# Two graph attention layers, 16 batches on one core: five places in another order, and the third values from rounded halves

## The chip, the core and the metric

The kernel runs on one core of a Trainium2 chip. Such a core has a matrix engine (TensorE, here PE, with its weight loads as PEld), a vector engine (DVE), a scalar engine (ACT), GpSimd (POOL) and a sequencer that only issues transfers (SyncE, SP). They run side by side and wait for each other through semaphores. The metric is the device time of one launch in microseconds, lower is better.

## The reference, cut to what matters

There are 16 batches of 512 nodes with 256 features. Each batch goes through a graph attention network of two layers (four heads, then one), a residual sum and a norm, and then through a third attention layer, a second residual and norm:

```python
def gat_layer(x, mask, W, a_src, a_dst, bias, concat):
    xl = (x @ W).reshape(B, N, H, F)
    asrc = jnp.einsum('bnhf,hf->bnh', xl, a_src)
    adst = jnp.einsum('bnhf,hf->bnh', xl, a_dst)
    e = leaky_relu(asrc[:, :, None, :] + adst[:, None, :, :], 0.2)
    e = jnp.where(mask[..., None], e, -1e9)
    attn = jax.nn.softmax(e, axis=1)          # over the sources
    out = jnp.einsum('bsdh,bshf->bdhf', attn, xl)
...
x1 = layernorm(x + gat_layer(elu(gat_layer(x, 4 heads)), 1 head))
Wh = x1 @ W                                   # the "third values"
e = leaky(s_i + s_j), masked; attention = softmax(e, axis=1)
out = layernorm(x1 + leaky(attention @ Wh))
```

## The kernel before

**Tiles.** The 512 nodes are four blocks of 128 partitions, and an attention map is a tile `att` of 128 x (4 x 512), three of them in turn. One map is a *unit*: a head ("h", four per batch), the second layer ("L2") or the third ("L3").

**The steady part.** Units are put into slots, six to a batch: in round n position 0 holds L3 of batch n-3, positions 1 to 4 the heads 0 to 3 of batch n, position 5 L2 of batch n-1. Each engine runs one loop over the slots (PE line 662, ACT 838, DVE 1171, POOL 431), and the order of the instructions within a slot is written out by hand, for each engine apart. Nothing reorders them: an engine that waits holds up all that stands behind.

**What a unit passes through.** PE spreads the source scores over PSUM (`sources_row`, L470 into bA). DVE takes the masked maxima over it (`tops`, four passes, L942), and from them the shifted targets (`shifted_targets`: low L955, b_t L960). PE spreads b_t (`targets_row`, L470 into bB). ACT applies the leaky slope (`leaky`, L734, two pairs) and the exponential (`exps`, L749). DVE clears what is no edge (`keep_edges`, L993). In the next slot PE multiplies the map with the values, in two halves (`attend`; heads L510, L2 L521, L3 L531). A head then goes through `invert` (DVE, L973), `normalize` (ACT, L761), `elu_exp` (ACT, L769), `elu` (DVE, L967), `turn_head` (PE, four transposes, L500), `high_part` (ACT, L775) and `low_part` (DVE, L979). The last L2 but one is already taken through exps and keep_edges in two halves (`halved_second`).

**Values.** The first values (`values_1`, L618 and L621) and the second (`values_2`, L603) are made of three matmuls each in a rounded format (fp32r): high x high, high x low, low x high. The third values (`values_3`, L591) are one full-precision product for each of two blocks of the contraction, which the profile shows as two matmul instructions. Before them `turn_x1` transposes x1 on PE (L582), and `x1_out` copies it out on ACT (L785). Products go through two banks bG; ACT copies them out (`values_1_out` L802, `values_2_out` L797, `values_3_out` L792).

**PE's order** in the positions that matter here, in round n:
- position 5: values_1 block 2; attend head 3, first half; turn_head; values_1 block 3; attend, second half; sources_row
- position 0: turn_x; attend L2, first half; turn_head; targets_row; attend L2, second half; sources_row
- position 1: attend L3, first half; turn_head; targets_row of head 1; values_1 block 0; attend L3, second half; sources_row
- position 3: values_2 blocks 2 and 3; attend head 1, first half; targets_row of head 3; turn_x1; attend, second half; sources_row of L2
- position 4: values_3 blocks 0 and 1; attend head 2, first half; turn_head; targets_row of L2; values_3 blocks 2 and 3; attend, second half; sources_row

**The rest.** `second_out` (DVE, L1020 and L1023) takes the second layer out of PSUM in two pairs and adds x; the statistics of both norms are `norm_stats` (DVE, L1032 and L1035), for the third layer at the end of position 4. POOL adds the bias to x (`add_bias_2`, L407), sets the diagonal (L421), adds the second residual (L429), writes the second norm (L390) and scales the third values (`scale_3`, L415). x_low (L1003) and make_mask (L998) run on DVE in position 0. After slot 96 comes a tail in which the last batch's layers follow one another with little beside them.

## Time and profile before

| | |
|---|---|
| median of three runs | 938.67 us (938.52 to 939.26) |
| the profiled execution | 939.34 us, span 937.1 us |
| granted TensorE clock, mean | 0.987 of full |
| PE busy | 874.0 us, 93% |
| PE's weight loads | 815.5 us, 87% |
| DVE busy | 753.4 us, 80% |
| ACT busy | 687.4 us, 73% |
| POOL busy | 258.1 us, 28% |
| moved by DMA | 45.03 MB |

Busy times overlap, so they don't add up. A matmul's end is modelled and reaches into the next one, so the distance between two starts tells what a group of matmuls takes, not the sum of their durations. The timeline merges instructions of one line that follow each other, and the bracket behind a row says how long the engine stood still before it and what it waited for.

### The profile page before, as it was taken

What the parts mean: (1) busy time and instruction counts of PE and PEld (TensorE: products, weight loads), DVE (VectorE), ACT (ScalarE), POOL (GpSimd) and SP (SyncE); (2) the same over time, 40 slices, a digit from 0 to 9 for tenths busy, and PEclk for the clock granted to TensorE, in tenths of its full rate; (3) what the DMA queues carried; (4) which work ended last, traced back from release to release, by engine and by line L of the source; (5) the groups of instructions that cost most, each with busy time, mean ns of one, the idle gap of its engine ahead of it and who ended that gap; (6) DMA issues with size and microseconds to landing.
All of it is one profiled execution on the core that took longest, in us unless ns stands there. A gap on an engine that the chain in (4) does not pass through costs nothing.

```text
span 937.1 us, 17310 instructions
## 1 busy us (share of the span) xinstructions
PE 874.0 (93%) x6220; PEld 815.5 (87%) x6220; DVE 753.4 (80%) x1908; ACT 687.4 (73%) x1274; POOL 258.1 (28%) x244
## 2 busy tenths in 40 slices
PE   6779889999999999999999999999999999999887
PEld 4778889998989989899998989999898998989775
DVE  6876788888788888878888887888888788887666
ACT  2686769687786877778687777868788686887653
POOL 1001020133242312434231243323224332332512
PEclk9898999999999999999999999999999999999999
DMA  7032030303013040300303021030301101000002
GB/s 217 25 106 76 1 90 2 90 2 111 3 33 81 3 111 2 85 30 25 89 1 113 2 48 65 23 92 1 114 1 46 68 23 23 1 24 1 24 1 68
DMA packets 62747, 45.03 MB, mean 48 GB/s; under 512 B 35780, under 2 KB 54340, under 8 KB 62664
## 3 DMA queue, kind: packets, MB, share of 16 engines
q1 hardware_dynamic: 62664, 43.93, 16.5%
q8 instruction: 51, 0.84, 0.4%
q14 instruction: 32, 0.26, 0.1%
HBM read 27.14 MB, written 8.39 MB: 38 GB/s over the span
## 4 chain that ended last, share of the span: by engine, by line
PE 38%; DVE 30%; ACT 23%; issue 9%; POOL 0%; DMA 0%; DVEq 0%; SPq 0%; POOLq 0%; ACTq 0%
DVE junk L942 9%; PE bUU L510 8%; PE bUU L531 7%; PE bG L603 6%; PE bG L621 6%; ACT att L734 5%; ACT att L749 5%; ACT x L761 4%; DVE y_lo L979 3%; PE bB L470 3%; DVE low L955 3%; DVE y L967 3%; DVE att L993 2%; ACT att L753 2%; DVE stats L1032 2%
## 5 line engine op out<-in xcount | busy, mean ns | idle before, releaser
L510 PE MATMUL bUU<-val,att 128*128 128x129 f32 x2048 | 249.2, 275 | 0.3 <-DVE att L993 0.3
L942 DVE CUSTOM_DVE_ANT_0 junk<-mask_t,bA,val 128x512 bf16<-128x512 bf16 x320 | 219.9, 743 | 33.9 <-PE bA L470 30.1
L510 PEld LDWEIGHTS bUU<-val,att 128*128 128x128 f32 x2048 | 241.4, 192 | 2.3 <-issue 0.5
L993 DVE SCALAR_TENSOR_TENSOR att<-mask_n,att 128x2048 f32<-128x2048 bf16 x78 | 178.8, 2292 | 79.3 <-ACT att L749 79.1
L734 ACT ACTIVATE att<-bB,val 128x512 f32<-128x512 f32 x320 | 202.7, 708 | 5.4 <-PE bB L470 5.4
L749 ACT ACTIVATE att<-att 128x2048 f32<-128x2048 f32 x78 | 151.5, 1942 | 0.6
L521 PE MATMUL bUU<-val,att 128*128 128x257 f32 x480 | 109.8, 381 | 1.9 <-DVE att L989 1.2
L531 PE MATMUL bUU<-val3s,att 128*128 128x256 f32 x480 | 109.2, 381 | 1.7 <-DVE res L1023 0.2
L381 POOL TENSOR_SCALAR var_eps<-moments 128x4 f32<-128x4 f32 x29 | 5.7, 195 | 368.1 <-DVE moments L1035 368.1
L802 ACT COPY val<-bG 128x524 f32<-128x524 f32 x62 | 37.6, 606 | 93.3 <-PE bG L621 93.3
L761 ACT ACTIVATE x<-bUU,zinv 128x128 f32<-128x128 f32 x256 | 73.4, 375 | 43.8 <-DVE zinv L973 43.8
L531 PEld LDWEIGHTS bUU<-val3s,att 128*128 128x128 f32 x480 | 89.1, 190 | 15.6 <-issue 4.0
L521 PEld LDWEIGHTS bUU<-val,att 128*128 128x128 f32 x480 | 88.7, 190 | 14.4 <-DVE att L989 1.5
L390 POOL TENSOR_SCALAR act<-res,moments,rstd 128x256 f32<-128x256 f32 x52 | 87.7, 1696 | 1.5
L603 PE MATMUL bG<-w_hi,y_hi 128*128 128x258 f32 x256 | 75.3, 294 | 0.3 <-DVE y_lo L979 0.3
L603 PE MATMUL bG<-w_hi,y_lo 128*128 128x258 f32 x256 | 72.4, 283 | 0.0
L621 PE MATMUL bG<-w_hi,x_hi 128*128 128x262 f32 x248 | 72.4, 292 | 0.0
L621 PE MATMUL bG<-w_lo,x_hi 128*128 128x262 f32 x248 | 72.3, 292 | 0.0
L603 PE MATMUL bG<-w_lo,y_hi 128*128 128x258 f32 x256 | 72.3, 282 | 0.0
L621 PE MATMUL bG<-w_hi,x_lo 128*128 128x262 f32 x248 | 72.1, 291 | 0.0
L470 PE MATMUL bB<-ident,b_t 128*128 128x128 f32 x320 | 50.7, 282 | 21.2 <-DVE b_t L960 21.1
L415 POOL TENSOR_SCALAR val3s<-val,z3inv 128x256 f32<-128x256 f32 x60 | 38.5, 657 | 98.3 <-DVE z3inv L1010 95.3
(126 smaller groups left out, 1635.8 us busy)
## 6 DMA issues: line engine op xcount, KB each, us to landing
adj_in<-in_adj_dram SPq DMA_DIRECT2D x16, 1024.0 KB, 5.8
x_in<-in_x_dram SPq DMA_DIRECT2D x16, 512.0 KB, 6.7
out_dram<-act SPq DMA_DIRECT2D x14, 512.0 KB, 2.9
mask_t<-mask_n SPq DMA_TRANSPOSE x64, 2.5
att<-in_L_gnn_W_dram SPq DMA_DIRECT2D x4, 128.0 KB, 3.1
val<-in_L_gnn_W_dram SPq DMA_DIRECT2D x1, 512.0 KB, 7.2
out_dram<-x_in SPq DMA_DIRECT2D x1, 512.0 KB, 2.9
w<-in_L_gnn_W_dram SPq DMA_DIRECT2D x1, 256.0 KB, 7.4
```

Of the source, the lines that this page charges most:

```text
L390: nc.gpsimd.tensor_scalar(act3[:, b], res2[:, b], moments[:, 1, b, 0:1], rstd[:, 1, b:b + 1], ALU.subtract, ALU.mult).then_inc(y_out_done, 1)
L470: ins = nc.tensor.transpose(bank[:, b * P:(b + 1) * P], column(b).to_broadcast([P, P]), ident[:])
L510: ins = nc.tensor.matmul(to[:, (d % 2) * FX:(d % 2 + 1) * FX], p[:, s, d * P:(d + 1) * P], val1[u.batch % 2][:, s, u.index // 2, values], ...
L521: ins = nc.tensor.matmul(to[:, 0:DO + 1], p[:, s, d * P:(d + 1) * P], val2[:, s, 2:DX + 1], start=(s == 0), stop=(s == NB - 1))
L531: ins = nc.tensor.matmul(to[:, d * DO:(d + 1) * DO], p[:, j, (2 * i + d) * P:(2 * i + d + 1) * P], val3s[:, j], start=(j == 0), stop=(j == ...
L603: ins = nc.tensor.matmul(g_bank(b % 2)[:, 0:DX], left[:, k, nodes], right[:, k], start=(k == 0 and i == 0), stop=(k == KH - 1 and i == 2))
L621: ins = nc.tensor.matmul(to, left[:, k, nodes], right[:, k, g], start=False, stop=(k == KD - 1 and i == 2))
L734: nc.scalar.activation(p[:, b], bB[:], ACT.Prelu, bias=a_col(u, b), alpha=SLOPE)\
L749: nc.scalar.activation(flat(p), flat(p), ACT.Exp).then_inc(exp_done, 1)
L761: nc.scalar.activation(x1[u.h % 2][:, d * P:(d + 1) * P], bU[u.use[d // 2] % 4][:, (d % 2) * FX:(d % 2) * FX + F], ACT.Copy, scale=zinv[u. ...
L942: nc.vector.tensor_tensor_reduce(junk[:, b] if u.row else att[u.slot % 3][:, b], mask_t[u.batch % 4][:, b], bA[:], 1.0, a_col(u, b) if u.r ...
L993: nc.vector.scalar_tensor_tensor(flat(p), mask_n[u.batch % 3][:, 0:NB * N], BIG, flat(p), ALU.add, ALU.min)\
```

## The change

1. ACT, position 5: `values_1_out` of block 2 stands before the second pair of leaky, not behind it.
2. DVE, position 1: the second pair of `second_out` stands behind tops and shifted_targets of the next head.
3. DVE: `norm_stats` of the third layer goes from the end of position 4 to position 5, behind invert.
4. POOL, position 3: `add_bias_2` waits until b_t of head 3 is there. POOL's order stays.
5. Every L2 is taken through exps and keep_edges in two halves, and attend waits for its own half; attend of L3 waits for the third values block by block.
6. Third values as three fp32r products. ACT rounds x1 (x1_hi), DVE subtracts (`x1_low`: x1_lo) in position 3, behind keep_edges, and twice in the tail. w3 is split once, at the start, by two more DVE instructions. PE waits for all of x1_lo before the first block.

The tiles and semaphores that the diff declares are left out here.

```diff
@@ -63,15 +63,19 @@
 
-    halved_second = units[LAST - 1]
     PARTS = (range(0, 2), range(2, 3), range(3, 4))
...
         u.r = i
+
+    pieces = 0
     for u in units.values():
         u.h = H * u.batch + u.index
+        u.p = pieces
+        if u.row:
+            pieces += 1 if u.kind == "h" else NB if u is final_second else 2
 
...
@@ -441,6 +451,8 @@
                 if pos == 3 and 0 <= n - 1 < B:
+
+                    pool.wait_ge(b_t_ready, units[SLOTS * n + H].r + 1)
                     add_bias_2(n - 1)
@@ -504,7 +516,7 @@
                 to = u_bank(u.use[i])
-                pe.wait_ge(prob_done, u.r + 1)
+                pe.wait_ge(prob_done, u.p + 1)
                 for d in range(2 * i, 2 * i + 2):
@@ -514,7 +526,7 @@
                 p = att[u.slot % 3]
-                pe.wait_ge(prob_done, u.r + 1 + (i if u is halved_second else 0))
+                pe.wait_ge(prob_done, u.p + i + 1)
                 for d in range(2 * i, 2 * i + 2):
@@ -525,9 +537,10 @@
                 to = u_bank(u.use[i])
-                pe.wait_ge(val3s_done, (u.batch + 1) * NB)
                 for d in range(2):
                     for j in range(NB):
+                        if i == 0 and d == 0:
+                            pe.wait_ge(val3s_done, u.batch * NB + j + 1)
                         ins = nc.tensor.matmul(to[:, d * DO:(d + 1) * DO], p[:, j, (2 * i + d) * P:(2 * i + d + 1) * P],
@@ -536,7 +549,7 @@
                 for s in sources:
-                    pe.wait_ge(prob_done, u.r + s + 2)
+                    pe.wait_ge(prob_done, u.p + s + 1)
                     for d in range(NB):
@@ -581,15 +594,16 @@
                     ins.then_inc(x1t_turned, 1)
-                    g_free[k] = ((x1t_ready, m * KD + k + 1),)
+                    g_free[k] = ((x1_hi_ready, m * KD + k + 1), (x1_lo_ready, m + 1))
 
...
                     g_wait(b % 2)
+                    pe.wait_ge(x1_lo_ready, m + 1)
                     for k in range(KD):
-                        pe.wait_ge(x1t_ready, m * KD + k + 1)
-                        ins = nc.tensor.matmul(g_bank(b % 2)[:, 0:DX], x1_t[:, k, b * P:(b + 1) * P], w3[:, k],
-                                               start=(k == 0), stop=(k == KD - 1))
+                        for i, (left, right) in enumerate(((x1_hi, w3_hi), (x1_hi, w3_lo), (x1_lo, w3_hi))):
+                            ins = nc.tensor.matmul(g_bank(b % 2)[:, 0:DX], left[:, k, b * P:(b + 1) * P], right[:, k],
+                                                   start=(k == 0 and i == 0), stop=(k == KD - 1 and i == 2))
                     ins.then_inc(val3_done, 1)
@@ -676,6 +690,8 @@
                 if pos == 4 and third:
+                    if n == 2:
+                        pe.wait_ge(w3_lo_ready, 1)
                     values_3(n - 2, (0, 1))
@@ -740,7 +756,7 @@
                 p = att[u.slot % 3]
-                if u is halved_second:
+                if u.kind == "L2":
                     act.wait_ge(leaky_done, (u.u + 1) * NB)
@@ -782,7 +798,7 @@
                     act.wait_ge(x1t_turned, m * KD + k + 1)
-                    nc.scalar.copy(x1_t[:, k], g_bank(k)).then_inc(x1t_ready, 1)
+                    nc.scalar.copy(x1_hi[:, k], g_bank(k)).then_inc(x1_hi_ready, 1)
 
@@ -853,6 +869,8 @@
                     normalize(older)
+                if pos == 5 and batch:
+                    values_1_out(n + 1, 2)
                 if this:
@@ -861,8 +879,6 @@
                     values_3_out(n - 2, (0, 1))
-                if pos == 5 and batch:
-                    values_1_out(n + 1, 2)
                 if this:
@@ -982,14 +998,14 @@
                 dve.wait_ge(diag_done, u.batch + 1)
-                if u is halved_second:
+                if u.kind == "L2":
                     mask = mask_n[u.batch % 3][:, 0:NB * N].rearrange("p (b n) -> p b n", n=N)
                     for i, half in enumerate((slice(0, N // 2), slice(N // 2, N))):
-                        dve.wait_ge(exp_done, u.r + i + 1)
+                        dve.wait_ge(exp_done, u.p + i + 1)
                         nc.vector.scalar_tensor_tensor(p[:, :, half], mask[:, :, half], BIG, p[:, :, half], ALU.add, ALU.min)\
...
                     return
-                dve.wait_ge(exp_done, u.r + 1)
+                dve.wait_ge(exp_done, u.p + 1)
                 nc.vector.scalar_tensor_tensor(flat(p), mask_n[u.batch % 3][:, 0:NB * N], BIG, flat(p), ALU.add, ALU.min)\
@@ -1002,6 +1018,11 @@
                                         x_hi[:].rearrange("p k n -> p (k n)"), ALU.subtract).then_inc(x_lo_ready, 1)
+
+            def x1_low(m):
+                dve.wait_ge(x1_hi_ready, (m + 1) * KD)
+                nc.vector.tensor_tensor(x1_lo[:].rearrange("p k n -> p (k n)"), bG[:],
+                                        x1_hi[:].rearrange("p k n -> p (k n)"), ALU.subtract).then_inc(x1_lo_ready, 1)
 
@@ -1130,6 +1151,10 @@
                     fold(w3[:, k, 2:DX], att3[:, DO:2 * DO], w3[:, k, 1:2])
+                nc.vector.tensor_copy(w3_hi[:], w3[:]).then_inc(w3_hi_ready, 1)
+                dve.wait_ge(w3_hi_ready, 1)
+                nc.vector.tensor_tensor(w3_lo[:].rearrange("p k n -> p (k n)"), w3[:].rearrange("p k n -> p (k n)"),
+                                        w3_hi[:].rearrange("p k n -> p (k n)"), ALU.subtract).then_inc(w3_lo_ready, 1)
 
@@ -1177,11 +1202,11 @@
                     invert(older)
+                if pos == 5 and 0 <= n - 3 < B:
+                    norm_stats(n - 3, 1, res2, res2_done, 2, stats2, moments2)
                 if g == LAST:
...
                     shifted_targets(thirds[END - 2])
-                if pos == 1 and units.get(g - 2):
-                    second_out(units[g - 2], 2)
                 if last_head:
@@ -1189,6 +1214,8 @@
                     second_out(units[g - 1], 0)
+                if pos == 1 and units.get(g - 2):
+                    second_out(units[g - 2], 2)
                 if this and not this.row:
@@ -1199,10 +1226,12 @@
                     x_low(n + 1)
-                if this is halved_second:
+                if g == LAST - 1:
                     invert(final_head)
...
                     keep_edges(this)
+                if pos == 3 and 0 <= n - 2 < B:
+                    x1_low(n - 2)
                 if oldest and pos != 1:
@@ -1211,18 +1240,17 @@
                     norm_1(n - 2)
-                if pos == 4 and 0 <= n - 3 < B:
-                    norm_stats(n - 3, 1, res2, res2_done, 2, stats2, moments2)
             second_out(units[SLOTS * B - 1], 2)
...
             norm_1(END - 1)
+            x1_low(END - 1)
             invert_3(END - 2)
...
                 p = att[final_second.slot % 3]
-                dve.wait_ge(exp_done, final_second.r + s + 2)
+                dve.wait_ge(exp_done, final_second.p + s + 1)
                 nc.vector.scalar_tensor_tensor(p[:, s], mask_n[END % 3][:, s * N:(s + 1) * N], BIG, p[:, s], ALU.add, ALU.min)\
@@ -1233,6 +1261,7 @@
             residual_2(END - 2)
+            x1_low(END)
             tops_by_targets(thirds[END])
```

What moves on DVE in position 1. `tops` are the rows `junk,top`, second_out is z2inv and res. Before, from the end of position 0 on:

```order
L967 SCALAR_TENSOR_TENSOR y_1<-e,x_1 128x512
L1020 RECIPROCAL z2inv<-bUU 128x1 x2
L1023 SCALAR_TENSOR_TENSOR res<-bUU,z2inv,x_in 128x256 x2
L942 ISA junk,top<-mask_t,bA,val_1 128x512
L942 ISA top 128x1
```

Here the second layer's pair is worked on before the four tops of head 1, of which the first is shown. After, on DVE in position 1, behind those four tops:

```order
L971 SCALAR_TENSOR_TENSOR low<-top,val_1 128x4
L976 SCALAR_TENSOR_TENSOR b_t<-top,low 128x4
L1041 RECIPROCAL z2inv<-bUU 128x1 x2
L1044 SCALAR_TENSOR_TENSOR res<-bUU,z2inv,x_in 128x256 x2
L1009 SCALAR_TENSOR_TENSOR att<-mask_n,att 128x2048
```

The pair now stands between b_t and keep_edges. DVE from b_t of head 3 in position 3 to the first top of L2 in position 4, before:

```order
L955 SCALAR_TENSOR_TENSOR low<-top,val_1 128x4
L960 SCALAR_TENSOR_TENSOR b_t<-top,low 128x4
L993 SCALAR_TENSOR_TENSOR att<-mask_n,att 128x2048
L967 SCALAR_TENSOR_TENSOR y_0<-e,x_0 128x512
L973 RECIPROCAL zinv<-bUU 128x2 x2
L942 ISA junk,top<-mask_t,bA,val 128x512
```

Between b_t and the next tops stand keep_edges, elu and invert. After, the same stretch of DVE:

```order
L971 SCALAR_TENSOR_TENSOR low<-top,val_1 128x4
L976 SCALAR_TENSOR_TENSOR b_t<-top,low 128x4
L1009 SCALAR_TENSOR_TENSOR att<-mask_n,att 128x2048
L1024 TENSOR_TENSOR x1_lo<-bG,x1_hi 128x1024
L983 SCALAR_TENSOR_TENSOR y_0<-e,x_0 128x512
L989 RECIPROCAL zinv<-bUU 128x2 x2
L958 ISA junk,top<-mask_t,bA,val 128x512
```

x1_lo has come in between keep_edges and elu. ACT in position 5, before (leaky in two pairs of `bB`, the copy of block 2, the exponential, the copy of block 3):

```order
L734 ACTIVATE att<-bB,val 128x512 x2
L761 ACTIVATE x_0<-bUU,zinv 128x128 x4
L734 ACTIVATE att<-bB,val 128x512 x2
L802 COPY val_0<-bG 128x524
L749 ACTIVATE att<-att 128x2048
L802 COPY val_0<-bG 128x524
```

The copy of block 2 stands behind both pairs. ACT in position 5, after:

```order
L750 ACTIVATE att<-bB,val 128x512 x2
L777 ACTIVATE x_0<-bUU,zinv 128x128 x4
L818 COPY val_1<-bG 128x524
L750 ACTIVATE att<-bB,val 128x512 x2
L762 ACTIVATE att<-att 128x4x256 x2
L818 COPY val_1<-bG 128x524
```

The copy stands ahead of the second pair, and the exponential has become two.

## Rows read from the trace of the kernel before

**Rows 1.** The page, busy time of PE: us (share of the span) xinstructions.
```profile
PE 874.0 (93%) x6220; PEld 815.5 (87%) x6220; DVE 753.4 (80%) x1908; ACT 687.4 (73%) x1274; POOL 258.1 (28%) x244
```

**Rows 2.** Waits of PE over the run: engine, line, waited for: us, times, longest.
```profile
PE bB L470 <- DVE b_t L960: 21.1, 30, 3.3
...
PE bG L618 <- ACT val L802: 10.3, 13, 1.4
```

**Rows 3.** Timeline, position 5: start us, us, engine, line, op, out<-in, xcount [idle <-releaser].
```profile
429.20 1.14 ACT L761 ACTIVATE x<-bUU,zinv 128x128 f32<-128x128 f32 x4 [1.78 <-DVE zinv L973]
...
430.79 0.60 PE L500 MATMUL bUU<-ident,y 128*128 128x128 f32 x4
...
432.13 0.36 PE L618 MATMUL bG<-bias,ones_r 128*128 128x262 f32 x1 [0.75 <-ACT val L802]
```

**Rows 4.** Timeline, position 1 of the batch before.
```profile
389.62 0.60 PE L470 MATMUL bA<-ident,val 128*128 128x128 f32 x4
...
390.36 3.69 PE L531 MATMUL bUU<-val3s,att 128*128 128x256 f32 x16
...
390.94 0.88 DVE L1023 SCALAR_TENSOR_TENSOR res<-bUU,z2inv,x_in 128x256 f32<-128x256 f32 x2
...
393.89 0.60 PE L500 MATMUL bUU<-ident,y 128*128 128x128 f32 x4
...
394.94 0.65 PE L470 MATMUL bB<-ident,b_t 128*128 128x128 f32 x4 [0.45 <-DVE b_t L960]
```

**Rows 5.** Timeline, end of position 2 to position 4.
```profile
409.98 0.37 PE L603 MATMUL bG<-w_hi,y_hi 128*128 128x258 f32 x1
...
412.70 2.36 POOL L407 TENSOR_TENSOR x_in<-x_in,bias 128x1024 f32<-128x1024 f32 x1
...
412.96 1.95 PE L510 MATMUL bUU<-val,att 128*128 128x129 f32 x16
...
413.06 2.02 DVE L955 SCALAR_TENSOR_TENSOR low<-top,val 128x4 f32<-128x4 f32 x1
...
413.43 1.91 ACT L749 ACTIVATE att<-att 128x2048 f32<-128x2048 f32 x1
...
415.33 0.65 PE L470 MATMUL bB<-ident,b_t 128*128 128x128 f32 x4 [0.43 <-DVE b_t L960]
...
415.45 2.29 DVE L993 SCALAR_TENSOR_TENSOR att<-mask_n,att 128x2048 f32<-128x2048 bf16 x1 [0.17 <-ACT att L749]
...
418.19 0.69 DVE L967 SCALAR_TENSOR_TENSOR y<-e,x 128x512 f32<-128x512 f32 x1 [0.44 <-ACT e L769]
...
418.92 1.91 PE L591 MATMUL bG<-w,x_t 128*128 128x258 f32 x8
...
420.67 1.95 PE L510 MATMUL bUU<-val,att 128*128 128x129 f32 x16
...
422.26 0.17 DVE L960 SCALAR_TENSOR_TENSOR b_t<-top,low 128x4 f32<-128x4 f32 x1
...
422.45 0.60 PE L500 MATMUL bUU<-ident,y 128*128 128x128 f32 x4
...
422.89 0.60 PE L470 MATMUL bB<-ident,b_t 128*128 128x128 f32 x4
```

**Rows 6.** Groups by line and shape: xcount | busy us, mean ns.
```profile
L1003 DVE TENSOR_TENSOR x_lo<-bG,x_hi 128x1024 fp32r<-128x1024 f32 x16 | 19.5, 1218 | 0.0
```

**Rows 7.** Timeline of the end.
```profile
888.09 1.27 ACT L785 COPY x_t<-bG 128x512 f32<-128x512 f32 x2
...
889.22 0.75 DVE L942 CUSTOM_DVE_ANT_0 junk<-mask_t,bA,val 128x512 bf16<-128x512 bf16 x1 [2.11 <-PE bA L470]
...
913.28 0.36 DVE L1035 BATCH_NORM_AGGREGATE moments<-stats 128x2 f32<-128x6 f32 x4
...
916.13 0.65 PE L470 MATMUL bA<-ident,val 128*128 128x128 f32 x4 [0.46 <-ACT val L792]
```

**Rows 8.** Timeline of DVE, the first tops of the run.
```profile
24.27 0.75 DVE L942 CUSTOM_DVE_ANT_0 junk<-mask_t,bA,val 128x512 bf16<-128x512 bf16 x1 [2.65 <-issue]
```

More of the change, by code:

```diff
@@ L111, in gat_kernel @@
         w3 = sb("w3", [P, KD, DX])
+        w3_hi = sb("w3_hi", [P, KD, DX], F32R)
+        w3_lo = sb("w3_lo", [P, KD, DX], F32R)
         bias2 = sb("bias2", [P, DO])
@@ L133, in gat_kernel @@
         x1n = [sb(f"x1n{i}", [P, NB, D]) for i in range(2)]
-        x1_t = sb("x1_t", [P, KD, N])
+        x1_hi = sb("x1_hi", [P, KD, N], F32R)
+        x1_lo = sb("x1_lo", [P, KD, N], F32R)
         act3 = sb("act3", [P, NB, D])
@@ L180, in gat_kernel @@
         w2_lo_ready = sem("w2_lo_ready")
+        w3_hi_ready = sem("w3_hi_ready")
+        w3_lo_ready = sem("w3_lo_ready")
         colsum_done = sem("colsum_done")
@@ L209, in gat_kernel @@
         val2_ready = sem("val2_ready")
-        x1t_ready = sem("x1t_ready")
+        x1_hi_ready = sem("x1_hi_ready")
+        x1_lo_ready = sem("x1_lo_ready")
         val3_ready = sem("val3_ready")
```

## The prediction

> **What bounds the kernel now.** I read the page first, for the shares of the engines, then PE's waits added up over the run, and then the timeline of one batch. The page has PE busy for 93% of the span [rows 1]. From about 200 us to 820 us the timeline of PE repeats itself batch by batch, and in each batch it stands still at the same few places. Summed over the run these are 13 waits for ACT's copy of values_1 (10.3 us) and 30 waits for the targets b_t from DVE (21.1 us) [rows 2]. Everywhere else the matmuls follow each other without a gap. So a microsecond counts if it is taken from PE's work, or from one of these waits with nothing else late behind it, and it costs if it makes PE wait anew. DVE and ACT matter by their order, not by their sum.
>
> The waits of a batch, measured from start to start (a matmul's modelled end hides some 0.15 us of a wait). Four transposes take 0.44 us, sixteen attention matmuls of a head 1.78 (starts at 420.67, 422.45 and 422.89) [rows 5].
> - Position 5: turn_head starts at 430.79, the next product at 432.13. 1.34 - 0.44 = **0.90 us**, waiting for ACT's copy of block 2 [rows 3].
> - Position 1: 389.62 to 390.36 is 0.74 for 0.44 of work, **0.30**, waiting for the scaled third values. 393.89 to 394.94 is 1.05 for 0.44, **0.61**, waiting for b_t, which DVE computes behind second_out [rows 4].
> - Position 3: 412.96 to 415.33 is 2.37 for 1.79, **0.58**, waiting for b_t. Its step before, low (L955), took 2.02 us and ended with POOL's add_bias_2 (L407, 412.70 to 415.06) [rows 5]. The same step takes 0.17 elsewhere.
>
> **The change part by part**, against the profiled run's own 939.34 us (span 937.1); the median of the three runs, 938.67, is 0.7 below it.
>
> *Position 5.* ACT now copies block 2 before the second pair of leaky. The products of that block are done two attention halves before PE needs the copy, and normalize, which stands ahead of the copy, waited 1.78 us for DVE's zinv [rows 3]. That is what norm_stats in front of invert cost, and the change puts norm_stats behind it. The wait of 0.90 should go in full. The exponentials of the second layer start no later than before (ACT does the same work in another order), and in halves they cost ACT and DVE some tenths that lie beside PE's products. Batches 3 to 14: 12 x 0.90 = 10.8. Batch 1's wait was longer, but b_t follows close behind: 0.8. **A = -11.6.**
>
> *Position 1.* The wait for the third values goes (PE starts with the first block; with position 5 repaired, z3inv is also earlier against PE). DVE's four tops now start when PE's sources row is there and not after second_out, whose two sums alone took 0.88 [rows 4], its reciprocals another 0.1: I put b_t 0.6 before PE asks for it. 11 x 0.91, plus 0.4 in batch 3 and 0.5 in batch 2, where the order helps but little. **B = -10.9.**
>
> *Positions 3 and 4.* Here three things meet. First, POOL now waits for b_t, so low takes 0.17 again: b_t is done at 413.06 + 0.36 = 413.42, and PE reaches it at 412.96 + 1.79 = 414.75, no wait. Second, PE's third values become three products. 24 such products took 412.96 - 409.98 = 2.98, 12 take 1.5, where the four full-precision products took 420.67 - 418.92 = 1.75 [rows 5]: 0.25 less twice a batch. Third, DVE gets x1_low between keep_edges and elu, 1.22 us by its twin x_low, of the same shape and operands [rows 6], and PE may not start values_3 before it. That chain hangs on ACT: exp (L749) ends at 413.43 + 1.91 = 415.34, and none of the edits moves it, since ACT comes to it from PE's second values. Keep_edges starts at 415.45 and takes 2.29 [rows 5]; x1_low would end at 418.88. PE, without a wait, would be there at 414.75 + 0.44 + 0.87 (turn_x1, eight transposes) + 1.79 + 0.44 = 418.29. A new wait of 0.66 with 0.07 of signalling.
> But POOL's add_bias_2 now starts at about 413.57 and holds until 415.93, across the start of keep_edges. Whether it holds keep_edges up, no row shows. The bounds are 0 and 0.33 us (its first 0.15 is start-up, as low ended 0.02 after POOL); I take 0.33, for low, the same kind of instruction with two operands in SBUF, was held to the end of the same POOL instruction. Then x1_low ends at T = 419.21.
> The Trainium skill ("SBUF — State Buffer", who interferes with whom) says that a DVE instruction with two SBUF inputs and a GpSimd one that reads SBUF exclude each other, whichever comes first. By that, keep_edges is held as well; the row of low agrees (2.02 us).
> After x1_low DVE goes on with elu, invert and the tops: in the trace 418.19 to 422.26 + 0.17, so 4.24 [rows 5]. It starts 0.08 before T, so b_t is ready at T + 4.16 and PE's row starts at T + 4.21 = 423.42. PE itself would be there at T + 0.07 + 1.5 + 1.78 + 0.44 = T + 3.8, a second new wait of 0.4. Before, that row started at 422.89: 0.53 later, less 0.25 for the second pair of blocks, is **+0.28 per batch**. So what this place gains by the 0.58 and by 0.5 of cheaper products, it gives back to DVE. 12 x 0.28 = 3.4. Batches 2 and 15 had no wait of 0.58 here, so each pays 0.86: 1.7. In batch 1 add_bias_2 is pushed onto a keep_edges that PE waited for: 0.35. **C = +5.4.**
>
> *The end.* Twice x1_low stands bare. For batch 14 it can start when x1_out ends, 888.09 + 1.27 = 889.36, and lasts until 890.6; the tops that PE waits for started at 889.22 [rows 7]: +1.4. For batch 15 it comes after the statistics, which end at 913.28 + 0.36 = 913.64: ends 914.8, four blocks at 0.73 and a last copy bring the sources row to 918.5, before 916.13 [rows 7]: +2.4. **D = +3.8.**
>
> *Nothing.* The two halves of w3 at the start are two DVE instructions of half x_low's length, and DVE stood for 2.65 us before the first tops [rows 8]. If that cover were gone, 1.3.
>
> Sum: -11.6 - 10.9 + 5.4 + 3.8 = -13.3. 939.34 - 13.3 = 926.0 in the profiled run, **925.4** as a median.
>
> **The rivals.**
> 1. *Keep_edges is not held* (0.33 less in 14 batches): 925.4 - 4.6 = 920.8. For it speaks only that no row shows this instruction behind a running POOL one.
> 2. *DVE's lateness is carried on.* From position 4 it may reach position 1, where b_t has 0.6 to spare. If all of x1_low's 1.22 arrives there, 0.62 comes back per batch: 12 x 0.62 = 7.4, 932.8. Against it: in position 0 ACT and DVE are led by PE's last half of head 3, which comes earlier than before.
> 3. *Slower.* If add_bias_2 comes in only behind keep_edges, it holds the next DVE instruction with two SBUF operands, elu's (L967), for up to its own length, 2.2 us, and b_t of position 4 and PE with it. Without any hold the sum is -17.9; so over 1.28 us of hold in each of 14 batches makes the kernel slower, and the full 2.2 gives 938.67 - 17.9 + 30.8 = 951.6. Against it: POOL's gate opens at 413.42, two microseconds ahead of keep_edges.
> 4. *The order does nothing:* other producers are as late as those that were moved. Half of A and B back, 936.7. In the rows each moved step has its operands early.
>
> **How the numbers follow.** Forecast 0.55, rival 1 0.20, rival 2 0.12, rival 3 0.05, rival 4 0.04; 0.04 remain for an end that hides half of D (923.5). The range leaves out rivals 3 and 4, and the edge of 2: 919.5 to 933. A run of this kernel can tell 0.2%, 1.9 us, from no change. Slower: rival 3 and a worse 2, 0.05. Same: 0.04, from rivals 2 and 4 at their worst. Faster: 0.91.
>
> **What would show it.** PE's waits for L802 and for val3s in the repeated part gone; low at 0.17 in every batch; new waits of PE, about 1.0 us in front of values_3 for x1_low and 0.4 for b_t of position 4; a batch 1.5 us shorter; keep_edges of head 2 at about 2.6 instead of 2.29 (2.29 would be rival 1, and y at over 1 us rival 3); from x1_out of batch 14 to the end 3.8 us more. The forecast is wrong if a wait of PE for b_t in position 1 stays, or if values_3 takes more than 1.6 us a pair.

## The result and the profile after

The changed kernel takes **922.88 us** (median of 4 runs, 921.34 to 923.75), the kernel before 938.6: a ratio of 0.983 (95%: 0.981 to 0.985). The forecast was 925.4. The profiled execution took 922.76 us against 939.34, span 920.9 against 937.1, so the launch took 16.6 us less where the sum of the prediction had 13.3.

The page and PE's waits of the changed kernel, which answer to [rows 1] and [rows 2] (L976 was L960, L605 was L591, L818 was L802, L1024 is `x1_low`):

```profile
PE 859.4 (93%) x6348; PEld 813.0 (88%) x6348; DVE 753.1 (82%) x1940; ACT 688.5 (75%) x1288; POOL 261.9 (28%) x244
```

```profile
PE bG L605 <- DVE x_lo L1024: 17.4, 16, 3.3
PE bB L482 <- DVE b_t L976: 11.5, 7, 2.6
```

Of the 13 waits for the copy at position 5 three short ones are left in this view (0.7 us in all, none between 190 and 800 us), those for b_t fell from 30 to 7, and 16 waits for x1_lo are new. The timeline at position 5 (against [rows 3]) and position 1 (against [rows 4]):

```profile
366.67 1.14 ACT L777 ACTIVATE x<-bUU,zinv 128x128 f32<-128x128 f32 x4 [0.91 <-DVE zinv L989]
...
369.14 0.60 PE L512 MATMUL bUU<-ident,y 128*128 128x128 f32 x4
...
369.50 0.37 PE L632 MATMUL bG<-bias,ones_r 128*128 128x262 f32 x1
```

```profile
382.21 0.60 PE L482 MATMUL bA<-ident,val 128*128 128x128 f32 x4
...
382.65 3.62 PE L544 MATMUL bUU<-val3s,att 128*128 128x256 f32 x16
...
386.10 0.60 PE L512 MATMUL bUU<-ident,y 128*128 128x128 f32 x4
...
386.54 0.60 PE L482 MATMUL bB<-ident,b_t 128*128 128x128 f32 x4
```

turn_head to the next product takes 0.36 us, where it took 1.34; PE's rows at position 1 stand 0.44 apart, where they stood 0.74 and 1.05 apart. Positions 3 and 4, against [rows 5]:

```profile
351.39 0.17 DVE L971 SCALAR_TENSOR_TENSOR low<-top,val 128x4 f32<-128x4 f32 x1
...
351.83 2.36 POOL L417 TENSOR_TENSOR x_in<-x_in,bias 128x1024 f32<-128x1024 f32 x1 [0.74 <-DVE b_t L976]
...
353.76 2.58 DVE L1009 SCALAR_TENSOR_TENSOR att<-mask_n,att 128x2048 f32<-128x2048 bf16 x1 [2.01 <-ACT att L765]
...
356.26 1.21 DVE L1024 TENSOR_TENSOR x_lo<-bG,x_hi 128x1024 fp32r<-128x1024 f32 x1
...
357.62 0.36 PE L605 MATMUL bG<-w_hi,x_hi 128*128 128x258 f32 x1 [0.86 <-DVE x_lo L1024]
...
360.93 0.60 PE L512 MATMUL bUU<-ident,y 128*128 128x128 f32 x4
...
361.25 0.16 DVE L976 SCALAR_TENSOR_TENSOR b_t<-top,low 128x4 f32<-128x4 f32 x1
...
361.47 0.65 PE L482 MATMUL bB<-ident,b_t 128*128 128x128 f32 x4
```

low is free again (0.17 us), keep_edges is held for 0.29 us by the add that now starts later, PE waits for x1_lo (four transposes to the next product: 1.46 us for 0.44), and b_t of position 4 costs it 0.10 (360.93 to 361.47). And the end, against [rows 7], with granted clocks of two stretches (columns: busy us and instructions of PE, PEld, DVE, ACT, POOL, then the clock as a share of 2.4 GHz, and DMA):

```profile
853.06 2.17 DVE L971 SCALAR_TENSOR_TENSOR low<-top,val 128x4 f32<-128x4 f32 x1
...
869.28 0.36 PE L605 MATMUL bG<-w_hi,x_hi 128*128 128x258 f32 x1 [1.59 <-DVE x_lo L1024]
...
894.53 0.39 PE L605 MATMUL bG<-w_hi,x_hi 128*128 128x258 f32 x1 [3.33 <-DVE x_lo L1024]
...
899.62 0.65 PE L482 MATMUL bA<-ident,val 128*128 128x128 f32 x4 [0.46 <-ACT val L808]
```

```profile
890.00:894.50 4.50, 1.20 (x10) 0.88 (x8) 3.39 (x10) 1.56 (x3) 3.42 (x6) 1.00 0.00 0
894.50:898.00 3.50, 3.47 (x17) 3.50 (x18) 0.00 (x0) 0.75 (x2) 0.16 (x1) 0.53 0.00 0
```

PE stands 3.33 us for the last x1_lo, and then runs its products near half the clock (0.53 is close to the lower level, 1.2 GHz) until 898.

To compare kernels I use one row: the start of the third layer's first matmuls at position 1 (390.36 in [rows 4]). It comes once per batch. "Period" below is the mean of the 12 distances between the first and the thirteenth of them, "end" the time from the thirteenth to the last instruction.

| kernel | median us | period | end |
|---|---|---|---|
| before | 939.3 | 55.15 | 105.5 |
| changed | 922.9 | 53.19 | 113.0 |
| k12_stats_only: before, and edit 3 alone | 922.0 | 53.56 | 106.8 |
| k9_nosplit_nogate: edits 1, 2, 3, 5 | 915.8 | 53.13 | 106.7 |
| k1_nosplit: edits 1 to 5 | 907.4 | 52.47 | 106.9 |
| k2_split_only: edit 6 alone | 951.3 | 55.61 | 111.5 |
| k3_nogate: all but 4 | 919.7 | 52.89 | 112.1 |
| k4_gate_y: all, 4 opened later | 917.9 | 52.89 | 112.6 |
| k5_no5: all but 1 | 924.7 | 53.30 | 112.7 |
| k6_no1: all but 2 | 934.3 | 53.99 | 111.4 |
| k10_no_stats: all but 3 | 938.3 | 54.47 | 112.2 |
| k11_no_stats_no5: all but 1 and 3 | 943.4 | 54.85 | 112.2 |
| k7_tail_low: all, last x1_low earlier | 920.9 | 53.21 | 112.2 |
| k8_best: k1 and a later add at the end | 905.0 | 52.47 | 103.5 |

The changed kernel against before: 12 x 1.96 = -23.6 in the repeated part, +7.6 at the end, -0.2 ahead of it. The part ahead of the first of these starts took between 169.0 and 172.6 us in the fourteen profiled executions, so a median can differ by some us from what period and end give. The edits are numbered as in the section on the change; medians of before in the runs' own comparisons were 939.3 to 939.6.

### The profile page after: what moved, and what is told of

It reads as the page before. It is cut to its first block, busy times and chain, and to the rows that moved or that the text cites. A ratio compares the mean times of both kernels' runs of the same rounds, so it can differ in the third digit from the quotient of the medians.

```text
span 920.9 us, 17599 instructions
## 1 busy us (share of the span) xinstructions
PE 859.4 (93%) x6348; PEld 813.0 (88%) x6348; DVE 753.1 (82%) x1940; ACT 688.5 (75%) x1288; POOL 261.9 (28%) x244
## 4 chain that ended last, share of the span: by engine, by line
PE 77%; DVE 13%; ACT 6%; issue 4%; DMA 0%; POOL 0%; SPq 0%; POOLq 0%; DVEq 0%; ACTq 0%
PE bUU L522 17%; PE bUU L533 11%; PE bUU L544 11%; PE bG L617 10%; PE bG L635 9%; PE bG L605 5%; ACT att L765 4%; PE bA L482 4%; PE bB L482 3%; DVE att L1009 3%; DVE junk L958 3%; PE bUU L512 3%; DVE x_lo L1024 2%; PE bG L632 2%; PE bG L585 1%
## 5 line engine op out<-in xcount | busy, mean ns | idle before, releaser
L1009 DVE SCALAR_TENSOR_TENSOR att<-mask_n,att 128x2048 f32<-128x2048 bf16 x64 | 150.8, 2356 | 73.0 <-ACT att L765 73.0
L765 ACT ACTIVATE att<-att 128x2048 f32<-128x2048 f32 x64 | 123.4, 1929 | 0.6
L533 PEld LDWEIGHTS bUU<-val,att 128*128 128x128 f32 x480 | 89.0, 191 | 15.5 <-DVE res L1044 2.3
L818 ACT COPY val<-bG 128x524 f32<-128x524 f32 x62 | 37.2, 601 | 79.3 <-PE bG L635 79.2
L400 POOL TENSOR_SCALAR act<-res,moments,rstd 128x256 f32<-128x256 f32 x52 | 91.3, 1764 | 1.5
L482 PE MATMUL bA<-ident,val 128*128 128x128 f32 x384 | 58.5, 275 | 6.7 <-DVE top L958 5.5
L439 POOL TENSOR_TENSOR res<-act,x1n 128x1024 f32<-128x1024 f32 x13 | 30.9, 2380 | 107.3 <-DVE x1n L1064 107.3
```

The source lines that it names most:

```text
L400: nc.gpsimd.tensor_scalar(act3[:, b], res2[:, b], moments[:, 1, b, 0:1], rstd[:, 1, b:b + 1], ALU.subtract, ALU.mult).then_inc(y_out_done, 1)
L482: ins = nc.tensor.transpose(bank[:, b * P:(b + 1) * P], column(b).to_broadcast([P, P]), ident[:])
L533: ins = nc.tensor.matmul(to[:, 0:DO + 1], p[:, s, d * P:(d + 1) * P], val2[:, s, 2:DX + 1], start=(s == 0), stop=(s == NB - 1))
L765: nc.scalar.activation(flat(p), flat(p), ACT.Exp).then_inc(exp_done, 1)
L1009: nc.vector.scalar_tensor_tensor(flat(p), mask_n[u.batch % 3][:, 0:NB * N], BIG, flat(p), ALU.add, ALU.min)\
```

## Experiments

### The moves without the split, and the split without the moves

**k1_nosplit** puts back the full-precision product in `values_3` and drops x1_low and the split of w3:

```diff
-                    pe.wait_ge(x1_lo_ready, m + 1)
-                        for i, (left, right) in enumerate(((x1_hi, w3_hi), (x1_hi, w3_lo), (x1_lo, w3_hi))):
+                        pe.wait_ge(x1_hi_ready, m * KD + k + 1)
+                        ins = nc.tensor.matmul(g_bank(b % 2)[:, 0:DX], x1_hi[:, k, b * P:(b + 1) * P], w3[:, k],
```

> The changed kernel with only its five moves in the order: the third values are again full-precision products, and neither x1_low nor the three-product form is there. Theory: the moves alone bring all of the gain (turn_head at pos 5 about -0.96 us per batch, pos 1 about -1.0), and the split takes some back: against the changed kernel 1.02 us of wait for x1_lo per batch go and 0.44 us of products come back, -0.58 x 14 = -8 us, and the tail loses its two waits for x1_lo (-1.1 and -3.9): 907 to 910 us. Rival (the shorter products pay for the wait, and the split is even): 920 to 926 us.

Measured: 907.39 us, ratio to before 0.966 (0.964 to 0.967). As the theory had it. Between 190 and 798 us the view of waits shows no wait of PE at all: the period of 52.47 is PE's own work. The kernel before waited 0.98 us per batch at position 5, 1.04 at position 1 (0.30, 0.61 and some smaller ones) and 0.63 at position 3, measured from start to start; that is 2.65 of the 2.68 us by which its period is longer.

**k2_split_only** is the reverse, the kernel before with edit 6 alone: the three-product form as in the diff of the change, and on DVE

```diff
                     keep_edges(this)
+                if pos == 3 and 0 <= n - 2 < B:
+                    x1_low(n - 2)
```

> The kernel before with only the third values as three products of rounded parts, x1_low in pos 3 ahead of low_part's follow-up as in the changed kernel. Theory: PE gains 0.44 us of products per batch, and its pace is set by the DVE chain behind it (b_t and tops), into which 1.22 us of x1_low are put; the steady part gains at most 0.44 x 14 = -6 us, and the tail loses 5 us by two waits for x1_lo: 935 to 942 us. Rival (the split is what makes the change fast): 925 to 930 us.

Measured: 951.34 us, ratio 1.012 (1.011 to 1.014), beyond the upper end of what I expected. The steady part did not gain, it lost 0.46 us per batch, most of it at position 5:

```profile
432.85 0.60 PE L506 MATMUL bUU<-ident,y 128*128 128x128 f32 x4
...
434.89 0.36 PE L625 MATMUL bG<-bias,ones_r 128*128 128x262 f32 x1 [1.44 <-ACT val L811]
```

2.04 us from turn_head to the product, against 1.34 in [rows 3], is 0.70 more: the 0.44 us that PE saves on products it waits longer for ACT, and 0.26 of x1_low's 1.2 us on DVE come through as well. Small waits at positions 3 and 4 make up the rest of the 0.46. So PE did not set the pace of the kernel before at this place; a chain through DVE and ACT did. The split costs 12 us on the old order and 15.5 on the new one (922.9 - 907.4: 12 x 0.72 in the repeated part and 6.2 at the end).

### POOL's gate

**k3_nogate** takes out the one line of edit 4, **k9_nosplit_nogate** does so where there is no split either:

```diff
-                    pool.wait_ge(b_t_ready, units[SLOTS * n + H].r + 1)
```

> The changed kernel without POOL's wait for b_t ahead of add_bias_2. Theory: keep_edges is no longer held (2.29 instead of 2.58 us) but low_part is again held (2.02 instead of 0.17 us), PE waits 0.58 us for b_t at its old place and reaches x1_lo that much later, so that wait shrinks by as much: 920 to 924 us, the gate buys nothing as long as x1_lo is waited for. Rival (the waits add up): 0.58 x 14 = +8, 930 us or more.

> The five moves without the split, and besides without POOL's wait for b_t ahead of add_bias_2. Theory: with no wait for x1_lo behind it, the 0.58 us that PE waits for b_t at pos 2 (low held by POOL's add) is paid in full: 907.4 + 0.58 x 14 = 915 to 916 us; the gate is worth 8 us here, and less than nothing (+0.27 us per batch) beside the split. Rival (the gate buys nothing in either): 907 to 909 us.

Measured: 919.68 us (ratio 0.979, 0.977 to 0.980) and 915.79 us (0.975, 0.973 to 0.976). Without the split the gate is worth 0.66 us per batch (k9 to k1), 8.4 us in all, as expected. Beside the split it costs 0.30 per batch: k3 is 3.2 us *faster* than the changed kernel, just outside my band: the theory names keep_edges at 2.29 us, but its sum lets the two waits cancel and leaves these 0.29 us out. From 349.75 (the attention matmuls ahead) to the first third value k3's PE takes 6.06 us, the changed kernel's 6.35 (351.27 to 357.62): the difference is the 0.29 of keep_edges.

**k4_gate_y** keeps the gate, but opens it with the next head's output, y, so that the add runs beside tops:

```diff
-                    pool.wait_ge(b_t_ready, units[SLOTS * n + H].r + 1)
+                    pool.wait_ge(y1_done, units[SLOTS * n + 1].h + 1)
```

> The changed kernel, with POOL's add_bias_2 waiting for the result of the next head's tops instead of b_t, so that it runs beside the tops and not beside keep_edges. Theory: keep_edges 2.29 instead of 2.58 us, x1_lo 0.29 us earlier, the wait for it 0.75 instead of 1.02 us: -0.29 x 14 = -4, 918 to 920 us (the case of the prediction in which keep_edges is not held). Rival: the wait is not set by keep_edges, or residual work behind add_bias_2 comes too late: 922.5 us or more.

Measured: 917.89 us, ratio 0.977 (0.975 to 0.978), at the lower edge of what I expected. The same place as above, 1.0 us earlier in this trace:

```profile
352.73 2.29 DVE L1009 SCALAR_TENSOR_TENSOR att<-mask_n,att 128x2048 f32<-128x2048 bf16 x1 [2.01 <-ACT att L765]
...
356.30 0.36 PE L605 MATMUL bG<-w_hi,x_hi 128*128 128x258 f32 x1 [0.57 <-DVE x_lo L1024]
...
356.83 2.37 POOL L417 TENSOR_TENSOR x_in<-x_in,bias 128x1024 f32<-128x1024 f32 x1 [6.76 <-DVE y L983]
```

keep_edges takes 2.29 again, PE waits 0.29 less for x1_lo, the period is 0.30 shorter. So the hold of keep_edges is POOL's add, and the wait for x1_lo hangs on keep_edges. The Trainium skill ("SBUF — State Buffer", "Who interferes with whom") tells of such an exclusion between a DVE instruction with two SBUF inputs and a GpSimd one that reads SBUF; the traces agree: keep_edges took 2.58 us with the add running at its start, and 2.29 without it.

### Which move does it

**k5_no5** undoes edit 1, **k6_no1** undoes edit 2:

```diff
-                if pos == 5 and batch:
-                    values_1_out(n + 1, 2)
                 if this:
                     leaky(this, (2, 3))
...
+                if pos == 5 and batch:
+                    values_1_out(n + 1, 2)
```

```diff
+                if pos == 1 and units.get(g - 2):
+                    second_out(units[g - 2], 2)
                 if last_head:
                     low_part(last_head)
...
-                if pos == 1 and units.get(g - 2):
-                    second_out(units[g - 2], 2)
```

> The changed kernel with only the copy at pos 5 (head 2's values of the next batch) back behind leaky on ACT, as before. Theory: PE's wait for that copy returns, turn_head at pos 5 takes 1.3 us or more again instead of 0.36: +0.96 x 12 and +0.8 = about +12, 934 to 936 us. Rival: the wait for x1_lo a place earlier shrinks when PE is later there, and the two do not add up: +6 or less, 929 us or below.

> The changed kernel with only pair 2 of the residual at pos 1 back ahead of tops on DVE, as before. Theory: b_t at pos 1 comes 0.6 us later and PE waits for it again (0.61 per batch), while the 0.30 to 0.4 of the val3s order stays gained: +0.6 x 11 = +7, 929 to 931 us. Rival: all of the 1.0 us of pos 1 comes back, +11, 933 to 935 us.

Measured: 924.71 us (ratio 0.984, 0.983 to 0.986) and 934.26 us (0.994, 0.993 to 0.995). Both theories fell, and both times lie in the bands of their rivals, though not by what the rivals say: in k5 the wait for x1_lo stayed at 1.03 us. ACT's early copy, to which I had given the repair of position 5, is worth 1.8 us in the changed kernel, not 12. Edit 2 is worth 11.4, not 7: at position 1 of k6 PE waits 0.71 us (1.15 between the starts below, less 0.44) where it waited 0.61 in [rows 4]. The 0.30 for the third values did not come back.

```profile
391.29 0.60 PE L512 MATMUL bUU<-ident,y 128*128 128x128 f32 x4
...
392.44 0.65 PE L482 MATMUL bB<-ident,b_t 128*128 128x128 f32 x4 [0.55 <-DVE b_t L976]
```

That left edit 3, the move of norm_stats. **k10_no_stats** undoes it, **k11_no_stats_no5** undoes it and edit 1, **k12_stats_only** makes it alone, in the kernel before:

```diff
                     invert(older)
+                if pos == 5 and 0 <= n - 3 < B:
+                    norm_stats(n - 3, 1, res2, res2_done, 2, stats2, moments2)
...
-                if pos == 4 and 0 <= n - 3 < B:
-                    norm_stats(n - 3, 1, res2, res2_done, 2, stats2, moments2)
```

> The changed kernel with only norm_stats back at the end of pos 4 on DVE, ahead of invert, as before (ACT's copy of block 2 stays early). Run k5_no5, the mirror image, lost 1.8 us of the 12 expected. Theory now: the two moves are two cures of the one wait at pos 5, and either is enough: zinv comes 1.7 us later, the copy comes right behind normalize and still in time for PE: 923 to 926 us. Rival (the move of norm_stats alone was what removed the wait, ACT's copy nothing): 932 to 936 us.

> The changed kernel with both put back: norm_stats in pos 4 ahead of invert on DVE, and the copy of block 2 behind leaky on ACT. Theory (either move alone takes the wait away): only now it returns, 0.9 to 1.0 us at pos 5 of each batch and 12 of them: 933 to 936 us. Rival (the wait was gone for another reason, for example because the wait for x1_lo gives ACT and DVE time to catch up): 924 to 927 us.

> The kernel before with one single edit: norm_stats moved from the end of pos 4 behind invert of pos 5 on DVE. Theory: zinv comes 1.7 us earlier, ACT's copy with it, and the 0.90 us that PE waited at pos 5 go; but second_out still stands ahead of tops at pos 1, and as in run k6_no1 an earlier PE waits there longer (up to 0.2): between -11 and -8 us, 928 to 931 us. Rival (ACT's copy behind leaky is the cause by itself): 938 to 940 us.

Measured: k10 938.31 us (ratio 0.998, 0.998 to 0.999), k11 943.39 (1.005, 1.003 to 1.006), k12 **922.04** (0.982, 0.980 to 0.983). All three lie outside their bands. My theory that either of the two moves cures position 5 fell as well: k10 ends up 15.4 us behind the changed kernel; per batch, PE waits 0.53 us more at position 5 there, 0.44 from there to the end of position 0 and 0.20 at position 1. The move of norm_stats, alone, gives the kernel before 17.3 us, about as much as the whole change does. DVE in the kernel before, at the end of position 4:

```profile
427.36 1.40 DVE L1032 BATCH_NORM_STATS2 stats<-res 128x6 f32<-128x256 f32 x4
428.68 0.36 DVE L1035 BATCH_NORM_AGGREGATE moments<-stats 128x2 f32<-128x6 f32 x4
428.96 0.20 DVE L973 RECIPROCAL zinv<-bUU 128x2 f32<-128x2 f32 x2
```

The same place in k12:

```profile
421.48 0.23 DVE L973 RECIPROCAL zinv<-bUU 128x2 f32<-128x2 f32 x2
421.63 1.39 DVE L1032 BATCH_NORM_STATS2 stats<-res 128x6 f32<-128x256 f32 x4
...
421.75 1.14 ACT L761 ACTIVATE x<-bUU,zinv 128x128 f32<-128x128 f32 x4 [0.20 <-DVE zinv L973]
...
424.91 0.60 PE L500 MATMUL bUU<-ident,y 128*128 128x128 f32 x4
...
425.26 0.37 PE L618 MATMUL bG<-bias,ones_r 128*128 128x262 f32 x1
```

norm_stats takes 428.96 - 427.36 = 1.60 us, and ACT's normalize waited 1.78 us behind it [rows 3], here 0.20. The period falls by 55.15 - 53.56 = **1.59**: the whole length of norm_stats lay on the path. PE pays for it in three places: 0.99 at position 5 (0.35 between these starts, 1.34 in [rows 3]), 0.30 for the third values at position 1 and, of the 0.61 for b_t there, 0.22; another 0.07 is in the attention half between them (3.53 before, 3.46 in k12). In k12 the wait for b_t is 0.39:

```profile
388.24 0.60 PE L500 MATMUL bUU<-ident,y 128*128 128x128 f32 x4
...
389.07 0.65 PE L470 MATMUL bB<-ident,b_t 128*128 128x128 f32 x4 [0.23 <-DVE b_t L960]
```

The two places belong to one lateness. ACT comes late out of position 5 and passes it on to position 1. The link is z3inv in position 0, which DVE makes from ACT's exponentials of the third layer. Before:

```profile
385.27 0.60 PE L500 MATMUL bUU<-ident,y 128*128 128x128 f32 x4
...
387.20 0.18 DVE L1010 RECIPROCAL z3inv<-z 128x4 f32<-128x4 f32 x1 [0.79 <-ACT att L753]
```

and in k12:

```profile
380.00 0.60 PE L500 MATMUL bUU<-ident,y 128*128 128x128 f32 x4
...
381.34 0.18 DVE L1010 RECIPROCAL z3inv<-z 128x4 f32<-128x4 f32 x1 [0.20 <-ACT att L753]
```

Against PE's turn_head it comes 1.93 us later before and 1.34 in k12, 0.59 less, which is 0.30 + 0.07 + 0.22. POOL scales the third values with it, and the instructions of DVE up to b_t of position 1 stand behind it.

### The end

**k7_tail_low** exchanges two statements of the tail:

```diff
-            residual_2(END - 2)
             x1_low(END)
+            residual_2(END - 2)
```

> The changed kernel with x1_low of the last batch ahead of residual_2 of the batch two before it on DVE; the steady part is untouched. Theory: x1_lo comes 1.3 us earlier in the tail, PE's idle time there falls from 3.33 to about 2.0 us, and the granted clock stays near 1.0 in the 24 products behind it (0.121 us each instead of 0.215), which gives another 1 to 1.4 us: 919.5 to 921 us. Rival (the idle time only moves to the next wait): 922.9 us, no change.

Measured: 920.92 us, ratio 0.980 (0.979 to 0.981). The wait fell from 3.33 to 2.13 us, as expected, but the clock did not hold, so that the time lies in the band although half of the theory failed:

```profile
890.98 1.04 PE L595 MATMUL bG<-ident,x_in 128*128 128x128 f32 x8
...
894.14 0.36 PE L605 MATMUL bG<-w_hi,x_hi 128*128 128x258 f32 x1 [2.13 <-DVE x_lo L1024]
```

```profile
894.00:897.50 3.50, 3.35 (x18) 3.39 (x19) 2.79 (x10) 0.75 (x2) 0.53 (x2) 0.63 0.00 0
```

From turn_x1 to the first attention transposes it is 899.25 - 890.98 = 8.27 us, against 899.62 - 890.16 = 9.46 in the changed kernel: 1.2 less, the wait alone.

**k8_best** starts from k1_nosplit and takes away the other new thing at the end, low being held in the last batch:

```diff
+            pool.wait_ge(res1_done, END * NB)
             add_bias_2(END)
```

> The five moves without the split, as k1_nosplit (907.4), and one more line: in the last batch POOL's add_bias_2 waits for the last sums of x1, so that it no longer runs beside low. Theory: low in the tail takes 0.17 instead of 2.17 us, the 1.9 us wait of PE for res falls to about 0.7: 906 us, 1.2 less. Rival: the residual of the last batch is then late: 907.4 or more.

Measured: **905.02 us**, ratio 0.964 (0.962 to 0.965), the fastest kernel of this study. The median is 2.4 us lower than that of k1_nosplit, and the end of the profiled run 3.4 us shorter, more than the 1.2 expected from the wait. In k1_nosplit:

```profile
842.80 2.17 DVE L962 SCALAR_TENSOR_TENSOR low<-top,val 128x4 f32<-128x4 f32 x1
...
845.86 2.97 PE L527 MATMUL bUU<-val,att 128*128 128x257 f32 x8 [1.89 <-DVE res L1030]
```

```profile
846.00:850.00 4.00, 4.00 (x15) 3.36 (x16) 2.41 (x7) 2.04 (x4) 0.00 (x0) 0.59 0.00 0
```

and in k8_best:

```profile
845.11 0.17 DVE L963 SCALAR_TENSOR_TENSOR low<-top,val 128x4 f32<-128x4 f32 x1
```

```profile
844.00:848.00 4.00, 4.00 (x21) 3.29 (x20) 3.70 (x13) 3.42 (x6) 0.94 (x1) 1.00 0.39 131
```

The wait of 1.89 us goes in full, and the stretch of near half clock behind it too: the clock stays at 1.00.

## Why the prediction was right, and where it was not

The total was 2.5 us off, the sign and the range held. By its steps it is less good. A, B and C come to -17.1 us where the repeated part gave -23.6. Of these 6.5 us 5.2 are 12 x 0.43 in the period itself, forecast 1.53 shorter (0.90 + 0.91 - 0.28) and measured 1.96 shorter; the rest are terms of single batches that lie outside the twelve periods. The end was mis-sized by 3.8 us the other way. That the two partly cancelled is luck, and the credit within the repeated part was given to the wrong edits.

*Position 5 (A).* Place and size hold: forecast 0.90 per batch, measured 0.98 (turn_head alone takes 0.36 here, not the 0.44 assumed). The prediction named both causes, ACT's order and norm_stats, and said that the wait would go in full; it did not ask which of them made it. The runs did: norm_stats alone removes it (k12), ACT's copy adds 0.11 per batch once norm_stats is away (k5), and without that it helps, but PE still waits (k10: 0.53 at position 5; k11: 1.68).

*Position 1 (B).* Forecast 0.91 per batch, measured 1.01: 0.30 ahead of the third layer's first matmuls, and 0.71 behind, where from their start to the second block of values 10.57 us (390.36 to 400.93) became 9.86 (382.65 to 392.51). The forecast gave 0.61 to the order of second_out. In k12, where that order is the old one, 0.22 of it is gone already. In the changed kernel that order is worth more: without it the period is 0.80 longer (k6). The half sentence "with position 5 repaired, z3inv is also earlier against PE" was the better part of it, and should have been followed: a producer that is late at one place is late at the next too.

*Positions 3 and 4 (C).* Forecast +0.28 per batch, measured +0.03 (12.11 us from the attention matmuls at 412.96 to those at 425.07 before, most often 12.13 or 12.14 after). The wait for x1_lo was met (0.99 forecast, 1.02 measured), so was the hold of keep_edges (0.33 and 0.29), and low at 0.17. The products of a pair took 1.53, not 1.5. The term that failed is the second new wait, for b_t of position 4: 0.4 forecast, 0.10 measured. The step behind it was "418.19 to 422.26 + 0.17, so 4.24". That stretch of the old trace held a short wait of DVE for PE's row (the reciprocals at 418.80, the first top only at 419.12), which is no work. In the new trace the same instructions run from 357.40 to 361.41, 4.01 us. 0.25 x 12 is 3.0 us of the miss.

*The end (D).* Forecast +3.8, measured +7.6. Batch 14's x1_low cost 1.1 (forecast 1.4), batch 15's 3.9 (forecast 2.4): the wait came as worked out, but the 24 products behind it ran, most of them, at a granted clock near half, so that it took 5.09 us from the first of them to the sources row (894.53 to 899.62) where the forecast had 3.7. The third part was not in the forecast at all: a later add now meets low in the last batch (2.17 us, 0.98 before) and PE waits 1.88 for the residual sums where it waited 0.70; with the half clock behind that (0.50 from 857.2 to 860.6) it comes to 2.4 us: 17.65 from the matmuls at 848.32 to turn_x1 at 865.97, before 15.26 (872.20 to 887.46). k12 shows that this comes with edit 3 alone (low 2.17 there as well), k8 that it can be had back.

*Rivals.* The first (keep_edges not held) named nearly the measured total, 920.8, by a mechanism that did not take place; k4 made it take place and gave 917.9. The second did not happen: at position 1 b_t stays in time. The third stayed away, since the gate opens 1.9 us ahead of keep_edges (351.83 and 353.76). The fourth fell with k12. What none of them said is that edit 6 makes the kernel slower, by 15.5 us on this order: the forecast had the costs in its terms C and D, but nowhere set them against leaving the split out. Its x1_lo wait and its tail add up to 1.02 x 14 + 5.0 = 19 us, its cheaper products bring 0.44 x 14 = 6, 13 of the 15.5 us measured.

*What is left.* The period of k11 (54.85) is 0.31 shorter than that of before (55.15), with norm_stats and the copy at their old places in both. Its PE waits 0.70 longer at position 5, 1.04 for x1_lo and 0.04 for b_t of position 4; 1.04 of waits at position 1 and 0.63 at position 3 are gone, and the products are 0.43 shorter. Most of what was cured at positions 1 and 3 came back at position 5, where norm_stats and the copy were late as before. Edit 5 was never taken out by itself, and what it is worth stays open; edits 1, 2 and 5 together are worth 0.43 per batch without the split (k12 to k9), as much as the wait for b_t at position 1 that k12 has left.

## What to carry to other kernels

Where several engines are scheduled by hand, take a wait of the bounding engine back to the instruction that is late, and then ask how long that instruction's own delay is: 1.6 us of statistics ahead of two reciprocals cost 1.6 us per batch, though the wait behind them at position 5 was 0.9 to 1.0, and the rest was booked at position 1 under other names. A dearer form of the same arithmetic that shortens the bounding engine (0.44 us) is only a gain if what it asks of the next engine (1.2 us of DVE) has a place that nobody waits for. Make such edits one by one: here one of six carried as much as all together, and one took back half of what the others could give.

## What the hardware showed that I had not expected

- Half clock after a short stand. Behind waits of PE of 3.33, 2.13 and 1.89 us the granted clock was 0.53, 0.63 and 0.59 in the stretches shown above, and in the first of them a product of 128x258 took 0.215 instead of 0.121 us. Behind waits of 1.59 us (869.28 in the changed kernel) and 1.84 us (892.83 in the kernel before) it was 1.00, as in the row at the end of this section. The stand of 1.89 us in k1_nosplit had another of 1.17 us some 8 us ahead of it; what decides is not settled by these runs. The second half of such a loss is not in the view of waits.
- POOL's add of two SBUF tiles (2.36 us) held both DVE instructions with two SBUF inputs that began while it ran: low went from 0.17 to 2.17 us and ended with the add, keep_edges from 2.29 to 2.58. Moved beside tops, it held neither (k4). POOL's part of the second norm (L390, 128x256, one SBUF tile and two columns as inputs) did not hold them: in the kernel before keep_edges began at 378.70 while one of these ran, and took 2.29 us. POOL's next one, which began at 378.97 beside it, took 3.12 us instead of 1.22.

The changed kernel behind its wait of 1.59 us, columns as above:

```profile
869.20:873.00 3.80, 2.25 (x17) 2.07 (x18) 3.13 (x12) 0.75 (x2) 1.84 (x4) 1.00 0.00 0
```
